# A two-layer LoRA kernel: the narrow columns of its second pair by seven products instead of one long sum

## The reference

```python
# layer 1 (cond): W 1024x1024, Wr 8x1024, A 8x16x1024, B 8x1024x16
base   = x @ W.T
logits = x @ Wr.T + 5.0 * one_hot(language)
topw, topi = top_k(logits, 2);  gates = one_hot(topi) weighted with softmax(topw)
h1 = base + 2.0 * sum_e gates[e] * (x @ A[e].T) @ B[e].T
# layer 2 (ffn): W 1024x1024, b, A 4x8x1024, Bm 4x1024x8, Wr 4x1024
gates2 = softmax(h1 @ Wr2.T)
out = x + h1 @ W2.T + b + 2.0 * sum_e gates2[e] * (h1 @ A2[e].T) @ Bm[e].T
```

## Time and profile before

| what | value |
|---|---|
| median of 3 runs | 323.02 us |
| the three runs | 322.94, 323.02, 324.08 us |
| span of the profiled execution | 321.9 us |
| TensorE (PE) busy | 318.2 us, 99% |
| weight loads (PEld) busy | 311.9 us, 97% |
| VectorE (DVE) busy | 262.5 us, 82% |
| ScalarE (ACT) busy | 128.2 us, 40% |
| granted TensorE clock, mean | 1.000 |

### The profile page before, as it was taken

One profiled execution on the slowest core, in us unless ns is written; L12 is line 12 of the kernel. 1 busy time (PEld: TensorE's weight loads), 2 busy tenths in 40 slices (PEclk: granted clock), 3 DMA queues, 4 the chain that ended last, 5 costly groups with the idle time before them and its releaser, 6 DMA issues.

```text
span 321.9 us, 5996 instructions
## 1 busy us (share of the span) xinstructions
PE 318.2 (99%) x2246; PEld 311.9 (97%) x2246; DVE 262.5 (82%) x609; ACT 128.2 (40%) x258; POOL 11.3 (3%) x13
## 2 busy tenths in 40 slices
PE   8999999999999999999999999999999999999996
PEld 5999999999999899899999999999999999999996
DVE  3999999798799778988968968878895987888543
ACT  3872836495147236325412503421251350333111
POOL 1001003700000000000000000000000000000000
DMA  7999000000000312700330150051025006002003
GB/s 266 419 404 290 3 2 0 2 0 2 0 2 0 132 24 46 260 3 0 109 154 1 60 201 0 0 191 70 0 74 187 0 21 239 0 0 110 24 0 130
DMA packets 10704, 27.59 MB, mean 86 GB/s; under 512 B 3166, under 2 KB 4702, under 8 KB 10688
## 3 DMA queue, kind: packets, MB, share of 16 engines
q1 hardware_dynamic: 10256, 26.83, 23.5%
q10 hardware_dynamic: 432, 0.53, 0.5%
HBM read 18.97 MB, written 8.39 MB: 85 GB/s over the span
## 4 chain that ended last, share of the span: by engine, by line
PE 98%; DMA 1%; DVE 0%; issue 0%
PE sums L1310 98%; DMA in<-part 1%; PE sums L1571 0%; DVE rows L1069 0%; DVE b_high L806 0%
## 5 line engine op out<-in xcount | busy, mean ns | idle before, releaser
L1310 PE MATMUL sums<-b_high,a_high 128*128 128x256 f32 (+1 forms) x224 | 45.3, 286 | 0.3 <-DVE b_high L806 0.3
L1310 PE MATMUL sums<-b_low,a_high 128*128 128x256 f32 (+1 forms) x224 | 45.2, 286 | 0.0
L1310 PE MATMUL sums<-b_high,a_low 128*128 128x256 f32 (+1 forms) x224 | 45.0, 286 | 0.0
L1310 PEld LDWEIGHTS sums<-b_high,a_high 128*128 128x128 f32 x224 | 34.7, 189 | 1.0 <-ACT a_high L549 0.8
L1310 PEld LDWEIGHTS sums<-b_low,a_high 128*128 128x128 f32 x224 | 34.7, 189 | 0.0
L1310 PEld LDWEIGHTS sums<-b_high,a_low 128*128 128x128 f32 x224 | 34.6, 188 | 0.0
L1310 PE MATMUL sums<-t_high,s_high 128*128 128x354 f32 x96 | 31.3, 326 | 0.0
L1310 PE MATMUL sums<-t_low,s_high 128*128 128x354 f32 x96 | 31.1, 324 | 0.0
L1310 PE MATMUL sums<-t_high,s_low 128*128 128x354 f32 x96 | 31.1, 324 | 0.0
L1069 DVE TENSOR_TENSOR rows<-sums,rows 128x354 f32<-128x354 f32 x48 | 24.4, 522 | 4.1 <-PE sums L1310 3.4
L1310 PE MATMUL sums<-ct_low,st_high 128*128 128x244 f32 (+1 forms) x80 | 25.6, 320 | 0.0
(11 more groups left out here) (151 smaller groups left out, 845.8 us busy)
## 6 DMA issues: line engine op xcount, KB each, us to landing
stage<-tokens SPq DMA_DIRECT2D x14, 512.0 KB, 4.0
out<-rows SPq DMA_DIRECT2D x14, 512.0 KB, 4.9
in<-part SPq DMA_DIRECT2D x7, 585.0 KB, 8.8
in<-part SPq DMA_DIRECT2D x4, 777.0 KB, 14.0
in<-part SPq DMA_DIRECT2D x4, 265.0 KB, 16.4
rows<-tokens SPq DMA_DIRECT2D x2, 512.0 KB, 13.6
out<-rows SPq DMA_DIRECT2D x3, 192.0 KB, 2.3
c_plain<-gate_proj SPq DMA_DIRECT2D x1, 544.0 KB, 18.0
```

Source lines behind the costliest of these rows:

```text
L1310: return nc.tensor.matmul(out_, lhs, rhs, start=start, stop=stop, skip_group_check=True)
```

## The change

The second pair takes the loop's path for its narrow columns: seven products instead of `tail`. So the narrow T1 to T4 have to be there earlier. T1, T3 and T2 are now made in the first pair, T4 at the head of the second. Each now has a block of `c_plain` of its own to lie in (`TN_PLACE`), and the order in which they are rounded is T2, T3, T1, T4. In the second pair the wide product P1 stands between the narrow P5 and the narrow P4, P5 comes forward behind P6, and `turn_u` moves behind P2. All subtractions stay on VectorE.

```diff
-        TN_ORDER = (T1, T3, T2, T4)
+        TN_PLACE = {T1: C11, T2: C22, T3: C12, T4: C21}
+        TN_ORDER = (T2, T3, T1, T4)
...
 # ScalarE, pair()
-                if not first:
+                steady = not first
+                if steady:
                     round_next(j, S4, p3_done)
                 if second:
                     round_tn(T1, t1n_made)
-                    round_tn(T3, t3n_made)
-
-                    act.wait_ge(narrow_ready, 2)
-                    round_tn(T2, t2n_made)
                 if steady:
 
                     act.wait_ge(tails_out, j)
-                    act.wait_ge(p1n_done, j - 1)
+                    act.wait_ge(p1n_done, j)
                     copy(narrow[:, 1, 0, :], narrow_bank(BANK_NA)).then_inc(r1n_read, 1)
...
                 if first:
                     round_next(j + 1, S2, p6_done)
+                    act.wait_ge(narrow_ready, 1)
+                    round_tn(T2, t2n_made)
                     round_next(j + 1, S3, p7_done)
+                    round_tn(T3, t3n_made)
...
 # VectorE, pair()
                 if second:
-
-                    dve.wait_ge(gate_again, 64)
-                    make_tn(C11, C12, C11, t1n_made)
-                    make_tn(C12, C22, C12, t3n_made)
-                    split_tn(T1)
-
-                    make_tn(C11, C22, C11, t2n_made)
                     split_tn(T3)
                 if steady:
+                    split_s(j, S1)
+                if second:
+                    split_tn(T1)
+                if steady:
+                    dve.wait_ge(r1n_read, j)
+                    dve.wait_ge(p6n_done, j)
+                    add_sums(narrow[:, 0, 1, :], narrow_bank(BANK_NB), narrow[:, 1, 0, :]).then_inc(u2n_read, 1)
+                if second:
+                    dve.wait_ge(t2n_made, 1)
+                    make_tn(C21, C21, C22, t4n_made)
...
                 ins.then_inc(v_turned, 1)
-
-                if turning:
+                if first:
+                    dve.wait_ge(gate_again, 64)
+                    make_tn(C11, C12, C11, t1n_made)
+
+                if turning or second:
                     split_s(j + 1, S2)
...
                 low_part(vt[ER2:2 * ER2, :, :], vt_plain[:, :, :], vt[0:ER2, :, :]).then_inc(vt_ready, 1)
-                if not steady:
+                if first:
                     add_r22()
-                if second:
-                    split_tn(T4)
+                    next_s(S1)
+                    next_s(S2)
+                    make_tn(C12, C22, C12, t3n_made)
+                    dve.wait_ge(t1n_made, 1)
+                    make_tn(C22, C22, C11, t2n_made)
                 if not last:
                     split_x(j + 1, 0)
-                if first:
-                    next_s(S1)
-                    next_s(S2)
...
+                if first:
+                    split_s(j + 1, S2)
+                    split_tn(T2)
                 if not last:
                     split_x(j + 1, 1)
-                if first:
-                    split_s(j + 1, S2)
-                    split_s(j + 1, S3)
                 dve.wait_ge(c_done, j + 1)
                 add_sums(rows[:, 0, wide_at(1)], bank(BANK_C), rows[:, 0, wide_at(1)]).then_inc(c_out, 1)
+                if first:
+                    split_s(j + 1, S3)
...
 # TensorE, narrow_products(j, second)
+                if second:
+                    pe.wait_ge(tn_split, TN_ORDER.index(T2) + 1)
                 pe.wait_ge(s_split, 4 * j + S_NO[S2])
                 narrow_of_s(BANK_NB, S2, tn_high[T2], tn_low[T2], True).then_inc(p6n_done, 1)
...
-                pe.wait_ge(u2n_read, j - 1)
+                pe.wait_ge(u2n_read, j)
+                if second:
+                    pe.wait_ge(tn_split, TN_ORDER.index(T3) + 1)
                 pe.wait_ge(s_split, 4 * j + S_NO[S3])
                 narrow_of_s(BANK_NB, S3, tn_high[T3], tn_low[T3], False).then_inc(p7n_done, 1)
...
+                if second:
+
+                    pe.wait_ge(a_out, j)
+                    product_1(j)
+                    pe.wait_ge(tn_split, TN_ORDER.index(T4) + 1)
+                    pe.wait_ge(x_split[1], j + 1)
...
 # TensorE, pair()
-                else:
-                    pe.wait_ge(tails_out, j)
-                    pe.wait_ge(x_split[0], j + 1)
-                    tail(0, range(KC))
-                    pe.wait_ge(x_split[1], j + 1)
-                    tail(1, range(KC)).then_inc(narrow_ready, 1)
```

More of the change, by code:

```diff
@@ L734, in pair @@
                     round_x(j + 1, 0)
-                if steady and not last:
+                turning = steady and not second and not last
+                if turning:
                     act.wait_ge(u_half_turned, j - 1)
@@ L1085, in pair @@
             def pair(j, first=False, second=False, last=False):
-                steady = not first and not second
-                turning = steady and not last
+                steady = not first
+                turning = steady and not second and not last
                 base = STEPS * j
@@ L1123, in pair @@
+                if steady:
+                    split_s(j, S4)
+                    dve.wait_ge(p7n_done, j)
                     add_sums(narrow[:, 1, 1, :], narrow_bank(BANK_NB), narrow[:, 1, 0, :]).then_inc(u3n_read, 1)
+                if second:
+                    split_tn(T4)
+                if steady:
                     next_s(S1)
-                    dve.wait_ge(u3n_read, j - 1)
-                    dve.wait_ge(p5n_done, j - 1)
+                    dve.wait_ge(u3n_read, j)
+                    dve.wait_ge(p5n_done, j)
@@ L1526, in pair @@
             def pair(j, first=False, second=False, last=False):
-                steady = not first and not second
-                turning = steady and not last
+                steady = not first
+                turning = steady and not second and not last
                 s_no = S_NO_FIRST if first else S_NO
                 if steady:
-                    narrow_products(j)
-                elif first:
+                    narrow_products(j, second)
+                else:
                     pe.wait_ge(x_split[0], 1)
@@ L1554, in pair @@
                     pe.wait_ge(cw_split, B11 + 1)
-                else:
+                if not first and not second:
                     pe.wait_ge(a_out, j)
-                of_x(BANK_A, 0, 0, cw_high[B11], cw_low[B11], True).then_inc(p1_done, 1)
+                if not second:
+                    product_1(j)
                 if first:
@@ L1566, in pair @@
                     product_5(j, first=True)
+                if second:
+                    product_5(j)
                 def turn_u():
@@ L1586, in pair @@
                 of_x(BANK_A, 0, 1, cw_high[B21], cw_low[B21], False).then_inc(p2_done, 1)
-                if last:
+                if second or last:
                     turn_u()
-                if not steady:
+                if first:
                     small_y()
@@ L1601, in pair @@
                 lora(BANK_A, 0, 0)
-                if second or last:
+                if last:
                     product_5(j)
@@ L1624, in pair @@
                 mixed(BANK_B, 1, 0).then_inc(b_done, 1)
-                if not turning:
+                if first or last:
                     product_3(j)
```

68 lines of the change are left out of this document (25 added, 43 removed).

## The result

The changed kernel takes 330.81 us (median of 5 runs, 330.63 to 331.32) against 323.17 (5 runs), a ratio of 1.0233 with a 95% interval of 1.022 to 1.0245: 7.6 us slower. The forecast was 329.0, the range 328.0 to 331.3.

A forecast was written before the change was run, and what follows sets the result against it. TensorE's matmuls bound the kernel before; now VectorE's queue up to u2n delays narrow P7. Losses of 7.1 less 1.2 saved, 5.9 net, taken as 6.0, turn 323.0 into 329.0 us; range 328.0 to 331.3.

The forecast's parts named there:

- 1.2 us of matmul work saved: Second pair: TensorE's work shrinks from 28.46 to 27.26 us, 1.2 us saved if TensorE never waits.
- 0.2 us lost ahead of the mix: First pair's mix: vt ready at 124.30, so it starts at 124.5 instead of 124.28, 0.2 us lost.
- 1.85, 2.4 and 2.55 us ahead of P1, P6 and P7: Second pair's narrow products: TensorE waits for the first tile's split, T2's split and the addition u2n, respectively.
- the sum from the start of P7: Second pair: narrow P7's start at 138.84 plus 23.3 us gives the pair's end at 162.1, against 156.15 before.
- three waits under 5 us together: Sign of a wrong prediction: the second pair's three TensorE waits for VectorE sum to under 5 us.
- the other way round: Check by adding waits: 0.2 + 1.85 + 2.4 + 2.55 + 0.1 = 7.1 lost, 1.2 saved, 5.9 net.
- P7 at 138.84, set by u2n: Second pair: VectorE's queue finishes the addition u2n at 138.64, so narrow P7 starts at 138.84.
- rival 1: TensorE's clock falls in the second pair's waits, costing time behind P7: 330.6 to 332.2, named 331.0 us; chance 0.20.
- u's copy, 0.1 us: Second pair's wide part: ScalarE rounds a tile just ahead of u's copy, leaving `small_y` about 0.1 us of wait.
- P4 without a wait: Second pair: T4 is split by 142.0 and narrow P4 comes at 143.5, so no wait.
- From the third pair on everything shifted by the same: Third pair onward: the loop's code in the same relative place, so all is shifted by 6.0 us.
- The bounds: What the trace doesn't show (gate columns' landing, matmul starts after waits, VectorE's step): together 328.2 to 330.2 without the clock.

The follow-up runs named there:

- vt first: Changed kernel with the first narrow subtraction (T1) behind vt's low part and the following addition on VectorE, instead of ahead of both: 331.16 us, ratio 1.0234.
- fillers: Changed kernel with 7, 10 and 11 matmuls on ones in the second pair, ahead of narrow P1, P6 and P7: 331.55 us, ratio 1.0258.
- the shorter one at full clock: Changed kernel with the splits of S1 and narrow T1 behind u2n, plus 7, 10 and 3 matmuls on ones in TensorE's waits: 330.31 us, ratio 1.0212.
- u2n early: Changed kernel with the splits of S1 and narrow T1 behind the addition u2n instead of ahead of it: 330.61 us, ratio 1.0225.
- one more: Changed kernel with one more narrow-block subtraction in VectorE's queue behind narrow T2, its result not used: 332.47 us, ratio 1.0285.
- GpSimd splits: Changed kernel with the four splits of the narrow T blocks on GpSimd instead of VectorE: 331.35 us, ratio 1.0253.
- first tile first: Changed kernel with the split of the second pair's first tile ahead of S1, S2, narrow T3 and T2 on VectorE: 331.3 us, ratio 1.0255.
- the two with wide products in the waits: Changed kernel with wide P1 and P6 ahead of narrow P6, S1's and T1's splits behind u2n: 328.48 us; with VectorE's order changed too: 328.98 us.

## Why the prediction was right, and where it was short

- *1.2 us of matmul work saved*: the work is so in the trace, 20.54 us from wide P1 to the third pair, without a gap. Right, and worth nothing: even without any T work the stretch took 57.20 us against 56.86, since 0.9 us ahead of P6 and 0.4 ahead of P7 stay.
- *0.2 us lost ahead of the mix*: 0.5, as the gate columns came 0.3 to 0.5 later than I took. It didn't count (vt first).
- *1.85, 2.4 and 2.55 us ahead of P1, P6 and P7*: 1.77, 2.40 and none. The first two are right in size, but not costs of their own; the sum from the start of P7 was the right way, and adding up waits only a check. The forecast named three waits under 5 us together as a sign that it is wrong, and with 4.2 (3.7 by the profile's idle times) that sign came. The third wait is not gone but filled: P6 and P2 at half clock took 2.56 us longer. With it the other way round still closes: 0.5 + 1.77 + 2.40 + 2.56, and 0.57 behind P7, less 1.1 saved, are 6.7.
- *P7 at 138.84, set by u2n*: 139.23, which is also where P2 at half clock ended. That the queue alone holds P7 there is shown by u2n's end in the run with fillers, by the longer queue and by the shorter one at full clock.
- *The clock, rival 1, chance 0.20*: it did fall, to 1.2 GHz, in the changed kernel and again in the runs u2n early, one more, GpSimd splits, first tile first and vt first; it did not in the two runs with fillers and the two with wide products in the waits. That idleness brings back the half rate is what the Trainium skill says (TensorE: Matmul & The Clock Gate, Part 1); the trace agrees, with 0.50 from 133.4 us on, late in the second of the two waits. The mechanism was as written there, P6 and P2 slowed in the shadow of VectorE's queue. Its price was mis-sized: 0.57 us behind P7, not 1.6 or more. I had taken the length of the start's slow phase as lying behind P7, while here the clock was low from about 133.4 to 140.2 us, most of it in the shadow.
- *u's copy, 0.1 us*: none. *P4 without a wait*: right.
- *From the third pair on everything shifted by the same*: to the last VectorE instruction, 0.11 us off. Behind it 1.1 us came on top, a term that the sum did not have.
- *The bounds*: the terms as listed add up to 328.5 to 330.1, not to 328.2 to 330.2. It changes nothing here.

The measured time is 1.8 us over the forecast: 0.17 of jitter at the start, 0.22 for P7's later start beside it, 0.5 for the clock less u's copy, 0.1 in the later pairs, 1.1 behind the last instruction, and 0.15 because before's median went from 323.02 to 323.17 with more runs, less the 0.46 by which the two profiled spans differ more (8.1) than the medians (7.64). So that the time lies in the range is in part luck. The range reached above 330.2 for the clock's sake, but what filled it there was for more than half the 1.1 us at the end, for which the forecast had no term; without them the time would have been 329.7. That rival 1's 331.0 lies nearer to the measured time than the forecast is luck too, since its own price was 0.57.

## What to carry to other kernels

Work that shortens the bounding engine is worth what it saves only if the helper that has to prepare it has time in that stretch; count the helper's queue operation by operation from its last fixed point to the one the bounding engine waits for, and take the start from there. Of several waits for one in-order queue only the last counts, so removing an earlier one buys nothing. Waits in a matmul stream have a second price, the clock. It can hide behind the first, as here, and then keep a shorter queue from paying, so read the clock of every single run and not of the profiled one alone. And a change of the code can move what lies behind the last instruction: look there too before a difference of a microsecond is put down to the mechanism.

## What the runs showed of the hardware

- TensorE fell from 2.4 to 1.2 GHz in mid-kernel where it stood still for 1.77 us, worked for 1.36 and stood still for 2.40. The granted clock was 0.50 from 133.4 to 140.2 us. With 7 and 10 matmuls on ones in the two waits it stayed at 1.00.
- How long it is low varies from run to run of one kernel: the changed kernel's mean clock was 0.990 in three runs and 0.995 in two.
- The column of the granted clock doesn't tell the low level at the start: it reads 1.00 from 0.78 to 3.95 us, where the warm-up's matmuls took 3.17 us for 3840 columns, 0.83 ns each; ones of the same kind, as fillers in mid-kernel, took 0.43.
- VectorE is slowed by GpSimd on SBUF: beside GpSimd's splits its subtraction of 128x1024 took 2.93 us instead of 1.22, one of 128x512 up to 2.59 instead of 0.68. GpSimd's own split of 128x976 took 1.91 to 2.50 us. VectorE's additions with one operand in PSUM kept their pace, 0.95 for two.
- Eight tiny VectorE instructions at the start cost 0.44 us on the median (323.37 to 323.81), 0.3 of them behind the last VectorE instruction in the profile.
